# Second attention's pair loop: one half of each projection per step, and the low part of the transposed probabilities ahead of the next row maximum

## The reference, cut to what matters

```python
x = x + jnp.tanh(g_xattn[1]) * _L1_xattn_ref(_layernorm(x, axis=-1), ctx_768, Wq, Wk, Wv, Wout, bout)

# _L1_xattn_ref: both batches of the context form one list of 308 keys
qh = _split_heads(jnp.einsum('bnq,qi->bni', x, Wq))          # 8 heads of 128
kh = _split_heads(jnp.einsum('bmc,ci->bmi', context, Wk))
vh = _split_heads(jnp.einsum('bmc,ci->bmi', context, Wv))
sim = jnp.einsum('hid,hjd->hij', qh, kh) * SCALE
mean = jnp.mean(sim, axis=-1, keepdims=True)
sim = (sim - mean) * ATTN_MATRIX_SCALE + mean
attn = jax.nn.softmax(sim, axis=-1)
out = jnp.einsum('hij,hjd->hid', attn, vh)                   # ... joined
return jnp.einsum('bni,iq->bnq', out, Wout) + bout
```

## Time and profile before

| | us |
|---|---|
| median of 3 runs | 1076.07 |
| lowest and highest | 1074.3, 1076.31 |
| profiled execution | 1077.43 |
| its span in the trace | 1075.7 |
| TensorE busy in it | 970.7 (90%) |
| VectorE, ScalarE, GpSimd busy | 542.4, 436.2, 421.0 |
| granted TensorE clock, mean | 0.955 of full |

### The profile page before, as it was taken

The page is one execution under the profiler, slowest core; times in us unless marked ns, Lnnn a source line. Parts: engine busy times, 40 slices in busy tenths (PEclk is TensorE's granted clock), DMA queues, the critical chain, the costliest instruction groups (busy, mean ns, idle before and its releaser), DMA issues.

```text
span 1075.7 us, 18153 instructions
## 1 busy us (share of the span) xinstructions
PE 970.7 (90%) x5884; PEld 783.3 (73%) x5885; DVE 542.4 (50%) x1186; ACT 436.2 (41%) x1316; POOL 421.0 (39%) x536
## 2 busy tenths in 40 slices
PE   5999999999997649999999996899999999989995
PEld 3599999999996625555555554698989899985662
DVE  7545454544444542222222235767676766553463
ACT  0255555455543212222222222555555655535442
POOL 5333334343432033433433434655554633331242
PEclk9899999999999569999999997999999999999887
DMA  9600000000000833111111113100000000000002
GB/s 295 246 1 2 1 0 1 2 2 1 0 1 1 330 115 98 45 43 39 39 45 43 39 34 123 43 20 11 21 10 20 20 1 2 1 2 1 0 1 79
DMA packets 29018, 47.73 MB, mean 44 GB/s; under 512 B 4494, under 2 KB 23106, under 8 KB 28706
## 3 DMA queue, kind: packets, MB, share of 16 engines
q1 hardware_dynamic: 25553, 37.68, 10.4%
q0 software_dynamic: 3408, 9.31, 3.2%
HBM read 37.68 MB, written 9.31 MB: 44 GB/s over the span
## 4 chain that ended last, share of the span: by engine, by line
PE 79%; DVE 8%; DMA 4%; issue 3%; ACT 3%; POOL 2%; POOLq 0%; DVEq 0%; SPq 0%; ACTq 0%
PE banks L1436 11%; PE banks L477 9%; PE banks L479 8%; PE banks L478 8%; PE banks L511 8%; PE banks L485 6%; PE banks L1475 6%; PE banks L496 6%; PE banks L503 3%; PE banks L626 2%; DMA region_b<-xn_rows,token_now 2%; PE banks L1646 2%; PE banks L343 2%; PE banks L1461 1%; PE banks L1274 1%
## 5 line engine op out<-in xcount | busy, mean ns | idle before, releaser
L1436 PE MATMUL banks<-W,region_b 128*128 x312 | 149.6, 603 | 0.6 <-ACT region_b L1483 0.6
L1191 POOL TENSOR_TENSOR region_a<-region_a,recip 128x512 f32<-128x512 f32 x64 | 66.6, 1041 | 177.5 <-DVE recip L806 177.5
L1036 ACT ACTIVATE region_a<-banks,negmax 128x154 f32<-128x154 f32 x256 | 96.2, 389 | 92.0 <-DVE negmax L800 89.5
L1226 POOL TENSOR_TENSOR region_a<-region_a,recip 128x640 f32<-128x640 f32 x64 | 80.3, 1255 | 125.2 <-DVE recip L912 123.4
L1522 DVE TENSOR_TENSOR region_b<-banks,region_a 128x512 f32<-128x512 f32 x78 | 53.9, 692 | 114.8 <-PE banks L1436 114.8
L1570 POOL TENSOR_TENSOR region_b<-region_b 128x512 f32<-128x512 f32 x39 | 49.4, 1266 | 148.7 <-DVE region_b L1522 146.6
L511 PE MATMUL banks<-region_a 128*128 128x128 f32 x768 | 96.5, 275 | 1.6 <-DVE oT_low L823 1.5
L511 PEld LDWEIGHTS banks<-region_a 128*128 128x128 f32 x768 | 91.0, 192 | 2.4 <-issue 1.7
L1436 PEld LDWEIGHTS banks<-W,region_b 128*128 128x128 f32 x312 | 55.4, 192 | 44.7 <-issue 43.6
L1499 ACT COPY region_b<-banks 128x512 f32<-128x512 f32 x39 | 22.9, 586 | 153.7 <-PE banks L1461 153.7
L1475 PE MATMUL banks<-region_a,region_b 128*128 x312 | 76.9, 389 | 6.6 <-issue 5.1
(11 more groups left out here) (240 smaller groups left out, 2383.7 us busy)
## 6 DMA issues: line engine op xcount, KB each, us to landing
W<-in_L_ffn_W SPq DMA_DIRECT2D x1, 8192.0 KB, 27.2
y_slots<-region_b SPq DMA_DIRECT2D x39, 128.0 KB, 1.7
region_a<-in_L_ffn_b SPq DMA_DIRECT2D x1, 4096.0 KB, 19.3
region_a<-in_L_ffn_W SPq DMA_DIRECT2D x1, 4096.0 KB, 30.3
region_b<-in_L_xattn_Wq SPq DMA_DIRECT2D x2, 1024.0 KB
xn_rows<-region_b SPq DMA_DIRECT2D x1, 2048.0 KB, 8.6
out<-x SPq DMA_DIRECT2D x4, 512.0 KB, 3.0
region_b<-in_L_xattn_Wk SPq DMA_DIRECT2D x2, 768.0 KB
```

The costliest lines, as they stand in the source:

```text
L1036: e = act.activation(pr[:, j, 0:L.keys], scores[:, g % 2, u, i * L.keys:(i + 1) * L.keys], ACT.Exp, bias=negmax[:, g % 2, j:j + 1], accum_ ...
L1191: pool.tensor_tensor(whole, pr[:, :, 0:split], rc.broadcast_to([P, L.hs, split]), ALU.mult)
L1226: pool.tensor_tensor(probs1[:, n % 2], probs1[:, n % 2], rc, ALU.mult).then_inc(sem("p_norm"), 1)
L1436: mm = pe.matmul(banks[:, 2 * r + part, :], xgT[:, r, k, :], w, start=(k == 0), stop=(k == DK - 1))
```

## The change

On TensorE every step now has the same load: the values of one head of a group rather than of two (`pe_pair_pv(g, u)`), and one projection or a half (four of eight chunks) of an output projection. Queries of groups 2 and 3 are projected in steps 0 and 1 of the pair's own iteration, group 0 and 1 of the next pair in steps 6 and 7, the input transposes come at the end of step 5. In step 7 the transposes come ahead of the next scores. On VectorE `probsT_rest` of step n-1 comes ahead of `row_max` of step n+1. Work on token rows moves by a step or two; ScalarE loses one wait ahead of `probsT_high`. Before the loop, keys 0 to 3 get their low parts ahead of `mixed_pair(0)`, ScalarE rounds `Wq` between the fourth and the fifth key unit, the low part of `Wq` is made half by GpSimd and half by VectorE, and the "r" units come ahead of the first projection. After the loop the second half of group 2's values is added.

```diff
-def pe_pair_pv(pe, g):
-    for u in range(2):
-        c = 2 * g + u
-        for i in range(3):
-            m = 3 * u + i if i < 2 else 2
-            mm = pe_split(pe, o_ps[:, u * PAIR:(u + 1) * PAIR], (V_high[:, c, i, :], V_low[:, c, i, :]),
-                          (pT_high[:, g % 2, m, :], pT_low[:, g % 2, m, :]), i == 0, i == 2)
-    mm.then_inc(sem("o2_ps"), 1)
-def pe_pair_out(pe, r, bank, groups_done):
+def pe_pair_pv(pe, g, u):
+    c = 2 * g + u
+    for i in range(3):
+        m = 3 * u + i if i < 2 else 2
+        mm = pe_split(pe, o_ps[:, u * PAIR:(u + 1) * PAIR], (V_high[:, c, i, :], V_low[:, c, i, :]),
+                      (pT_high[:, g % 2, m, :], pT_low[:, g % 2, m, :]), i == 0, i == 2)
+    if u == 1:
+        mm.then_inc(sem("o2_ps"), 1)
+def pe_pair_out(pe, r, bank, chunks, groups_done):
     rows = slice(r * P, (r + 1) * P)
-    for c in range(NC):
-        if c == 0:
-            pe.wait_ge(sem("o2_sb"), groups_done - 1)
+    for c in chunks:
         if c == NC - 2:
             pe.wait_ge(sem("o2_sb"), groups_done)
         mm = pe_split(pe, bank[:, 0:D], (oT_high[:, c, rows], oT_low[:, c, rows]),
                       (Wo_high[:, c, :], Wo_low[:, c, :]), c == 0, c == NC - 1)
-    mm.then_inc(sem("y_ps"), 1)
+    if c == NC - 1:
+        mm.then_inc(sem("y_ps"), 1)
...
     pe_pair_x(pe)
-    pe.wait_ge(sem("Wq_split"), 1)
+    pe_kv1(pe, "r")
+    pe.wait_ge(sem("Wq_split"), 2)
     pe.wait_ge(sem("xt2_sb"), 1)
     pe_pair_q(pe, 0)
-    pe_kv1(pe, "r")
-    pe.wait_ge(sem("kv1_sb"), KV1_BEFORE_R)
+    pe.wait_ge(sem("kv1_sb"), KV1_BEFORE_R + 2)
     pe.wait_ge(sem("q2_sb"), 1)
     pe_pair_scores(pe, 0)
     pe_pair_q(pe, 1)
-    pe.wait_ge(sem("kv1_sb"), KV1_BEFORE_R + 2)
...
+        group = 4 * i
+        def transposes(n):
+            s = 8 * i + n
+            if not (first and n == 0):
+                pe.wait_ge(sem("p_norm"), s0 + s)
+                if not (first and n == 1):
+                    pe.wait_ge(sem("pt2_low"), s - 1)
+                pe_pair_probsT(pe, (n - 1) % 8)
+        def next_scores(n):
             s = 8 * i + n
             if not (last and n == 7):
                 if n % 2 == 1:
                     pe.wait_ge(sem("q2_sb"), 4 * i + (n + 1) // 2 + 1)
                 if not (first and n == 0):
                     pe.wait_ge(sem("p_exp"), s0 + s)
                 pe_pair_scores(pe, (n + 1) % 8)
+        def values(n):
+            s = 8 * i + n
             if n % 2 == 1 and not (first and n == 1):
                 pe.wait_ge(sem("pt2_low"), s - 1)
                 if not (first and n == 3):
+                    pe.wait_ge(sem("o2_sb"), group + n // 2 - 1)
+                pe_pair_pv(pe, (n // 2 - 1) % 4, 0)
+            if n % 2 == 0 and not (first and n in (0, 2)):
+                pe_pair_pv(pe, (n // 2 - 2) % 4, 1)
+        next_scores(0)
+        transposes(0)
+        pe.wait_ge(sem("q2_sb"), 4 * i + 2)
+        pe_pair_q(pe, 2)
+        values(0)
+        next_scores(1)
+        transposes(1)
+        pe.wait_ge(sem("q2_sb"), 4 * i + 3)
+        pe_pair_q(pe, 3)
+        values(1)
+        next_scores(2)
+        transposes(2)
+        if not first:
+            pe.wait_ge(sem("q2_sb"), 4 * i + 4)
+            if isinstance(i, int) and i == 1:
+                pe.wait_ge(sem("Wo1_split"), 2)
+            pe_pair_out(pe, 0, misc_ps, range(0, 4), None)
+        values(2)
+        next_scores(3)
+        transposes(3)
+        if not first:
+            pe_pair_out(pe, 0, misc_ps, range(4, NC), 4 * i)
+        values(3)
+        next_scores(4)
+        transposes(4)
+        if not first:
+            pe.wait_ge(sem("y_done"), t0 + 2 * i - 1)
+            pe_pair_out(pe, 1, misc_ps, range(0, 4), None)
+        values(4)
+        next_scores(5)
+        transposes(5)
+        if not first:
+            pe_pair_out(pe, 1, misc_ps, range(4, NC), 4 * i)
+        values(5)
+        if not last:
+            if first:
+                pe.wait_ge(sem("q2_sb"), 4)
+            else:
+                pe.wait_ge(sem("y_done"), t0 + 2 * i)
+            pe.wait_ge(sem("xn_ready"), t0 + 2 * i + 4)
+            pe_pair_x(pe)
+        next_scores(6)
+        transposes(6)
+        if not last:
+            pe.wait_ge(sem("xt2_sb"), i + 2)
+            pe_pair_q(pe, 0)
+        values(6)
+        transposes(7)
+        next_scores(7)
+        if not last:
+            pe.wait_ge(sem("q2_sb"), 4 * i + 5)
+            pe_pair_q(pe, 1)
+        values(7)
...
     pair_bodies(pe, L1, emit)
     pe.wait_ge(sem("p_norm"), s0 + STEPS)
     pe.wait_ge(sem("pt2_low"), STEPS - 1)
     pe_pair_probsT(pe, 7)
+    pe_pair_pv(pe, 2, 1)
     pe_stage(pe, *EARLY[0], 0)
     pe.wait_ge(sem("pt2_low"), STEPS)
     pe.wait_ge(sem("o2_sb"), GROUPS - 1)
-    pe_pair_pv(pe, 3)
+    for u in range(2):
+        pe_pair_pv(pe, 3, u)
     pe_stage(pe, *EARLY[1], 0)
     pe.wait_ge(sem("y_done"), t0 + NT - 2)
-    pe_pair_out(pe, 0, misc_ps, GROUPS)
-    pe_pair_out(pe, 1, o_ps, GROUPS)
+    pe_pair_out(pe, 0, misc_ps, range(NC), GROUPS)
+    pe_pair_out(pe, 1, o_ps, range(NC), GROUPS)
...
     dve_kv1(dve, L1, "v")
+    dve_kv1(dve, L1, "k", range(0, 4))
     mixed_pair(0)
-    dve_kv1(dve, L1, "k")
+    dve_kv1(dve, L1, "k", range(4, NC))
     dve.wait_ge(sem("rstd_in"), 3)
     dve_normalize(dve, 0, xn)
     dve_normalize(dve, 1, xn_odd)
+    pair_x_rest(1)
     dve.wait_ge(sem("Wq_high"), 1)
-    dve.tensor_tensor(Wq_low[:], Wq[:], Wq_high[:].bitcast(F32), ALU.subtract).then_inc(sem("Wq_split"), 1)
-    pair_x_rest(1)
+    dve.tensor_tensor(Wq_low[:, 1], Wq[:, 1], Wq_high[:, 1].bitcast(F32), ALU.subtract)\
+        .then_inc(sem("Wq_split"), 1)
+    dve_kv1(dve, L1, "r")
     mixed_pair(2)
     pair_q_rest(1, 0)
-    dve_kv1(dve, L1, "r")
     row_max(0, 0)
     pair_q_rest(2, 1)
...
             reciprocals(n, s)
+            if not (first and n == 0):
+                probsT_rest((n - 1) % 8, s - 1)
             if not (last and n == 7):
                 row_max((n + 1) % 8, s + 1)
-            if not (first and n == 0):
-                probsT_rest((n - 1) % 8, s - 1)
...
-            if n in (5, 6) and not first:
-                stats_of(dve, 2 * i + n - 7, "out", slot=n - 5)
-            if n in (6, 7) and not first:
-                aggregate(dve, 2 * i + n - 8, "out", None, slot=n - 6)
-            if n in (4, 6) and not (isinstance(i, int) and i < 2):
-                early = 2 * i - 4 + (n - 4) // 2
+            if n in (5, 7) and not first:
+                stats_of(dve, 2 * i + n // 2 - 4, "out", slot=n // 2 - 2)
+            if n == 6 and not first:
+                aggregate(dve, 2 * i - 2, "out", None, slot=0)
+            if n == 0 and not (first or is_body(i, 1)):
+                aggregate(dve, 2 * i - 3, "out", None, slot=1)
+            if n in (2, 4) and not (first or is_body(i, 1)):
+                early = 2 * i - 4 + (n - 2) // 2
                 dve.wait_ge(sem("rstd_out"), OUT + early + 1)
                 first_cur(dve, early)
-            if first and n in (1, 2):
-                pair_q_rest(n + 2, n + 1)
-            if n == 1 and not first:
-                pair_q_rest(4 * i + 4, 3)
-            if n in (2, 3) and not first:
-                add_y(dve, L1, 2 * i + n - 4, n - 2, misc_ps[:, 0:D])
-            if n == 4 and not last:
+            if n < 2:
+                pair_q_rest(4 * i + n + 3, n + 2)
+            if n in (3, 5) and not first:
+                add_y(dve, L1, 2 * i + n // 2 - 3, n // 2 - 1, misc_ps[:, 0:D])
+            if n == 5 and not last:
                 pair_x_rest(i + 2)
-            if n > 4 and not last:
-                pair_q_rest(4 * i + n, n - 5)
-            if n % 2 == 1 and not (first and n == 1):
-                o_rest((n // 2 - 1) % 4, 4 * i + n // 2 - 1)
+            if n > 5 and not last:
+                pair_q_rest(4 * i + n - 1, n - 6)
+            if n % 2 == 0 and not (first and n in (0, 2)):
+                o_rest((n // 2 - 2) % 4, 4 * i + n // 2 - 2)
...
+    dve.wait_ge(sem("stats_out"), t0 + NT - 2)
     probsT_rest(7, STEPS - 1)
+    o_rest(2, GROUPS - 2)
+    aggregate(dve, NT - 3, "out", None, slot=1)
...
-    act_kv1(act, L1, "k")
+    act_kv1(act, L1, "k", range(0, 4))
     act.wait_ge(sem("wq_in"), 32)
     act.copy(Wq_high[:], Wq[:]).then_inc(sem("Wq_high"), 1)
+    act_kv1(act, L1, "k", range(4, NC))
     x_high(1)
+    act_kv1(act, L1, "r")
     pair_q_high(1, 0)
-    act_kv1(act, L1, "r")
     act.wait_ge(sem("pads_zero"), 2)
...
-                if n % 2 == 1 and not (first and n < 5):
-                    act.wait_ge(sem("o2_ps"), 4 * i + n // 2 - 1)
                 probsT_high((n - 1) % 8, s - 1)
             if not (last and n == 7):
                 exponentials((n + 1) % 8, s + 1)
-            if first and n in (1, 2):
-                pair_q_high(n + 2, n + 1)
-            if n == 1 and not first:
-                pair_q_high(4 * i + 4, 3)
-            if n == 4 and not last:
+            if n < 2:
```

(26 more changed lines are left out.)

57 lines of the change are left out of this document (14 added, 43 removed).

## The result

The changed kernel takes 1090.55 us (median of 4 runs, 1090.23 to 1090.75) where the kernel before, run beside it, takes 1076.19 us (1074.3 to 1079.92). The ratio is 1.0129, interval 1.0102 to 1.0156: slower by 1.3%. Its profiled execution took 1090.23 us, span 1088.3, against 1077.43 and 1075.7. The forecast was 1081.1, range 1072 to 1090: the direction held, the time lies 0.55 us outside the range.

A forecast was written before the change was run, and what follows sets the result against it. It took TensorE, 90% busy, to be held only by the order in which results come. -4.5 us to iteration 0's end, +8.0 (iterations 1 to 5), +1.2 (6), +0.3 (7): +5.0 on 1076.07, so 1081.1 us, range 1072 to 1090.

The forecast's parts named there:

- what goes: TensorE's gaps ahead of transposes in steps 1 and 5 and the projection behind would vanish: -3.15 us per iteration.
- the chain and its waits: Transposes to next reader of `misc_ps` takes 5.4 us, before 3.83; new TensorE waits sum to 4.7 us per iteration.
- Rival B: Chain shorter than the forecast's links, 5.0 us rather than 5.4; iteration back to 34.7 us, total 1071; chance 0.15.
- A: Rival: the loop's three waits go and nothing follows, 31.5 us per iteration, total 1051.5; chance 0.08.
- D: Rival: GpSimd stretches VectorE's `mix`, 0.5 us twice per iteration, 6 us more, total 1087; chance 0.15.
- C: Rival: gain before the loop and loss in it cancel within 0.2%, iteration +0.7 us, total 1076; chance 0.10.
- Iteration 0 keeps its length within 1.4 us: First loop iteration: its length set by two GpSimd pieces of 2.37 us and the normalisations in GpSimd's queue.
- the first scores: Start of the loop's first scores, waiting for "r" and `mixed_pair(2)`: at 671.5 instead of 676.60, -5.1 us.
- the held mixes: Ahead of the loop, GpSimd's half of Wq's low part may hold `mixed_pair(0)`'s last `mix`: 2 us of gain lost.
- the gap of 3.93 us: TensorE's wait for keys' low part before the loop, then 7.8 us at half rate instead of 4.1; both go.
- a sign that the forecast gave for being wrong: At the loop's start: a loop that begins later than 676 us would show the forecast wrong.
- the end: Iteration 7: +2.3 us until the last transposes, -1.4 in the gap before group 3's values, -0.6 behind; sum +0.3.

The follow-up runs named there:

- e1: Changed kernel with the row maximum put back ahead of the low part on VectorE in every step: 1057.06 us, ratio 0.9822.
- The step experiments: Two kernels: the changed kernel with the row maximum first in steps 0 and 1 only (1079.11 us), or in step 6 only (1074.38 us).
- e10: e9 with "r" units ahead of the input transposes, and on VectorE their and Wq's low parts ahead of the input rows' low part: 1047.32 us.
- the experiment with step 6: Changed kernel with the row maximum first in step 6 only: 1074.38 us, ratio 0.9987.
- the second experiment: Kernel before with only VectorE's order changed, the low part ahead of the row maximum: 1099.48 us, ratio 1.0219.
- e9: e1 with Wq's low part whole on VectorE, `add_y` ahead of `mix`, Wo's low part later, first queries' low part ahead of `mixed_pair(2)`: 1048.14 us.

## Why the prediction was right or wrong, point by point

**Right: what goes.** The three waits of an iteration went as they stood, in the kernel after and in e1.

**Right: the chain and its waits.** Steps 5, 6, 7, 1 and 2 were forecast at 1.2, 0.27, 1.6, 1.05 and 0.55 us. From start to start the trace of after has, in the same order, 1.2, 0.27, 1.6, 1.05 and 0.54. The first of them (same timeline as above):

```profile
810.91 0.32 PE L603 MATMUL banks<-ident,xn 128*128 128x128 f32 x1 [1.06 <-DVE x L910]
```

The step experiments show that they hang on the order, one by one; e1 that nothing but the order makes the chain 5.40 us instead of 3.83. Iterations 1 to 6: +9.2 forecast, +9.4 measured. Rival B (a shorter chain) and A (nothing follows) fall by the 5.40 us; D (GpSimd stretches `mix`) has no room in the 36.3. C fell as well: the gain ahead of the loop doesn't reach the loss.

**The step that failed: "Iteration 0 keeps its length within 1.4 us".** It took 38.37 us, +4.2. I reasoned that GpSimd's queue sets this iteration and that waits of TensorE would vanish in it. Up to step 3 that holds: its transposes wait 3.06 us for GpSimd, they start 16.2 us after the first scores in both after and e1, and later pieces of Wo's low part took 2.9 us out. But behind that point GpSimd no longer sets anything, and I didn't walk the chain through the second half. There (TensorE, then the copy and the low part that needs it, kernel after):

```profile
690.15 0.77 PE L626 MATMUL banks<-ident,region_a 128*128 128x128 f32 x5 [3.06 <-POOL region_a L1270]
...
699.70 0.36 PE L477 MATMUL banks<-pT_high,V_high 128*128 128x256 f32 x1 [2.31 <-DVE oT_low L964]
...
708.90 0.41 PE L477 MATMUL banks<-K_high,q_high 128*128 128x308 f32 x1 [1.42 <-DVE q_low L938]
...
698.25 0.58 ACT L1144 CAST oT_high<-banks 128x512 fp32r<-128x512 f32 x1
...
698.86 0.69 DVE L964 TENSOR_TENSOR oT_low<-banks,oT_high 128x512 fp32r<-128x512 f32 x1 [1.26 <-ACT oT_high L1144]
```

Three terms, each against e1's iteration 0. The values of the next group overwrite the outputs' bank and wait for `oT_low`, whose copy stands behind the exponentials: 2.31 us against 0.61, so 1.7. In the later iterations TensorE has half an output projection to do in each of the two steps between, and this wait doesn't show. The scores of step 7 wait for `q_low` as in every iteration: 1.4. And the clock: after the idle 2.31 us, from 701.1 to 704.6 us, TensorE ran at its lower level (1.2 GHz), which it doesn't in e1.

```profile
701.00:704.00 3.00, 3.00 (x17) 2.97 (x14) 1.20 (x4) 1.59 (x5) 2.54 (x3) 0.53 0.16 44
```

The scores and transposes took 2.60 us there (701.26 to 703.86), 1.65 in e1 (698.40 to 700.05), and the next three matmuls 0.3 more: 1.25. With 0.28 for a wait for exponentials and 0.53 less for GpSimd that is 4.1 of the 4.4 us between the two kernels. I had left all three out of the sum for this iteration: the wait on the outputs' bank, the scores' wait and the lower clock.

**Mis-sized: the first scores.** Forecast -5.1 us, measured -3.28. The input transposes began at 661.96, forecast 661.8, and the held mixes were counted in. The "r" units behind them were taken at full rate; they took 5.10 us at half rate (granted clock 0.52 in the window of 660 to 665), where eight such matmuls at full rate take 3.43 us (e10's). Their low parts, and not the first projection, are what VectorE's second `mixed_pair` and behind it the first queries' low part stand behind (kernel after):

```profile
669.35 0.86 DVE L453 TENSOR_TENSOR V_low<-banks,V_high 64x256 fp32r<-64x256 f32 x2 [1.19 <-ACT V_high L432]
670.24 1.92 DVE L817 SCALAR_TENSOR_TENSOR x<-W,weight,x 128x256 f32<-128x256 f32 x4
```

By this chain the half rate is worth up to 1.7 of the missing 1.8 us, an estimate. The forecast knew the half rate from before, took it as gone with the gap of 3.93 us, and moved work behind the gap that replaced it. How long the clock stays low here differs between the profiles. The same units behind the same idle time, in the experiment with step 6:

```profile
L412 PE MATMUL banks<-region_b,ctx_rem x8: 592/828/1061, 661.1 to 665.8; 96*128 96x512 f32 x8
```

There the lower clock lasted from 661.1 to 664.5 us, in after from 660.2 to 667.1. Seven kernels have this code and the same idle time of 3.98 or 3.99 us. In the three profiles where the lower clock was short (both step experiments and the new stretch alone) the first scores come at 30.5 us, in the four where it was long (after, e1, `add_y` ahead of `mix`, Wo's low part later) at 31.3 to 31.7. So some 0.8 us of the miss is such scatter. The kernel before has it too: its code in the second experiment reached the first scores at 32.9 us instead of 34.6. And a sign that the forecast gave for being wrong came true: the loop proper, with the scores at 677.79, begins later than 676 us (before: 679.27), as a wait of 4.00 us for the first `q_low` and 3.5 us at the lower clock lie right ahead of it.

**Mis-sized: the end.** Forecast +0.3, measured +1.05, and the parts differ more than the sum. Up to the last transposes it was forecast at +2.3 us and is +2.7. The gap from them to the values of group 3 was to shrink by 1.4 us and stays, 3.70 us against 3.79: the half of group 2's values that was moved into it has its own copy and low part, and the values behind wait for that `oT_low`. What comes behind was forecast at -0.6 and is -1.6, with the clock at its full level there.

```profile
961.06 0.55 PE L477 MATMUL banks<-pT_high,V_high 128*128 128x256 f32 x1 [2.31 <-DVE oT_low L964]
...
966.82 0.36 PE L477 MATMUL banks<-pT_high,V_high 128*128 128x256 f32 x1 [0.62 <-DVE oT_low L964]
```

**Not touched by the change.** 1.2 us (0.66 ahead, 0.6 behind) of the 12.6 lie in code that the change doesn't touch. The start of this stage differs by up to 6 us between the profiles of all kernels here, and it goes with the clock: TensorE had spent 47.8 us at the lower level until then in the kernel that starts it first (638.6 us) and 64.9 in the one that starts it last (644.6). Over the twelve profiles the correlation is 0.95, at 0.35 us of start for each us at the lower level. Most of the difference lies in the first 80 us (granted clock in the second experiment and in e9):

```profile
0.00:80.00 80.00, 65.97 (x356) 49.34 (x358) 51.69 (x138) 25.14 (x99) 35.98 (x49) 1.00 0.53 183
```
```profile
0.00:80.00 80.00, 65.37 (x310) 48.00 (x312) 47.88 (x133) 23.02 (x88) 34.62 (x47) 0.91 0.53 182
```

No experiment sets it, so that the clock is the cause is not shown.

## What to carry to other kernels

When two instructions on an in-order engine may go either way, put first the one whose inputs are there already, and count who waits behind both: here the maximum fitted into VectorE's wait for ScalarE's copy, and setting it behind cost 1.57 us for everything that ScalarE has queued behind the exponentials, 24 to 33 us over the kernel. When a chain through four engines is forecast, walk it through the first and the last iteration too, as buffers are filled there in another rhythm: here the two ends held 8.8 of the 33 us that the order costs. A split of work between VectorE and GpSimd is worth something only when neither is held by the other meanwhile.

## What the hardware showed that I had not expected

A wait of 2.31 us in iteration 0 was followed by about 3 us at the lower level (granted clock 0.53 from 701 to 704 us), with matmuls of 308 columns 0.26 us apart instead of 0.14; this added 1.25 us to the wait, half its length again. But the length of a wait doesn't tell whether the clock falls. The kernel of the second experiment has two waits of 2.2 to 2.4 us in every iteration from 1 to 5, and its granted clock stays at the full level throughout. In e9 three short waits within nine us (0.99, 0.82 and 0.87 us) were followed by 3.5 us at the lower level. An iteration of the first, and that stretch of the second:

```profile
746.44:783.95 37.51, 32.48 (x262) 31.56 (x261) 24.48 (x52) 18.46 (x49) 18.82 (x24) 1.00 0.05 15
```
```profile
693.60:697.10 3.50, 3.50 (x18) 3.47 (x17) 1.95 (x5) 1.70 (x5) 3.02 (x4) 0.51 0.13 37
```

What decides is open; no run here separates it. The time of one and the same kernel goes with the clock too: over 39 executions of the kernel before, from 1071.07 to 1080.09 us, the mean granted clock lies between 0.948 and 0.959 of full, and its correlation with the time is -0.81.

A delay of 1.57 us at ScalarE came out at GpSimd's normalisation one step on (2.4 us of waiting in the second experiment), where the timeline names an engine that had been idle for 2.86 us.
